# A macaron block on one core: an order table and a scatter loop changed in the second feed-forward pass

## What is computed

```python
x = x + 0.5 * _L0_ffn_ref(_layernorm(x, axis=-1), ...)
x = x + _L0_attn_ref(_layernorm(x, axis=-1), ...)
x = x + 0.5 * _L0_ffn_ref(_layernorm(x, axis=-1), ...)
```

```python
logits = x @ wr.T + rb
probs = jax.nn.softmax(logits, axis=-1)
scores, idx = jax.lax.top_k(probs, TOP_K)
scores = scores / scores.sum(axis=-1, keepdims=True)
...
out = shared_out
for e in range(E_ROUTED):
    out = out + w[..., e:e + 1] * _expert(x, rg[e], ru[e], rd[e])
```

## Time and profile before

| what | us |
|---|---|
| median of three runs (627.84, 629.61, 633.13) | 629.61 |
| the profiled execution | 629.03 |
| its span, first to last instruction | 627.2 |
| PE busy | 565.7 (90%) |
| DVE busy | 456.2 (73%) |
| ACT busy | 330.2 (53%) |
| POOL busy | 257.0 (41%) |

### The profile page before, as it was taken

How to read it: one execution, slowest core, us unless ns; L and a number is a source line. 1 busy time by engine, 2 the same in 40 slices (tenths; PEclk the granted TensorE clock), 3 DMA queues, 4 the chain that set the end, 5 groups by cost and what they waited for, 6 DMA issues and landing times.

```text
span 627.2 us, 11848 instructions
## 1 busy us (share of the span) xinstructions
PE 565.7 (90%) x3738; PEld 431.5 (69%) x3738; DVE 456.2 (73%) x1139; ACT 330.2 (53%) x703; POOL 257.0 (41%) x404
## 2 busy tenths in 40 slices
PE   2969999998895789999999999999999899899995
PEld 1859899997863455555555555555556898899894
DVE  3677777778558978787878787787555677577865
ACT  4444444457433346666666666566775524344543
POOL 7387846445333511212121212121316888744440
PEclk9999999999976989999999999999999979899998
DMA  9913237732571462505050404020000031421403
GB/s 261 279 44 82 74 96 185 189 103 72 159 224 54 148 136 68 159 2 160 1 158 2 157 2 158 4 92 1 3 2 22 31 83 48 115 73 41 121 31 106
DMA packets 46888, 58.74 MB, mean 94 GB/s; under 512 B 6183, under 2 KB 37678, under 8 KB 46062
## 3 DMA queue, kind: packets, MB, share of 16 engines
q1 hardware_dynamic: 38160, 46.77, 26.5%
q0 software_dynamic: 4480, 9.25, 4.7%
q10 hardware_dynamic: 4190, 1.98, 1.3%
HBM read 38.09 MB, written 28.00 MB: 105 GB/s over the span
## 4 chain that ended last, share of the span: by engine, by line
PE 66%; DVE 13%; issue 8%; DMA 4%; POOL 4%; ACT 3%; SPq 2%; DVEq 0%; ACTq 0%; POOLq 0%
PE psum L1566 11%; PE psum L1609 10%; PE psum L1631 10%; PE psum L846 4%; DVE mxp L1713 4%; PE psum L864 4%; PE psum L848 4%; PE psum L847 4%; PE psum L882 4%; PE psum L885 3%; DMA queries<-m_rows 2%; PE psum L1569 2%; POOL z_rows L1104 2%; PE psum L905 1%; DVE at_l L1005 1%
## 5 line engine op out<-in xcount | busy, mean ns | idle before, releaser
L1713 DVE TENSOR_REDUCE mxp<-psum 128x1 f32<-128x512 f32 (+3 forms) x304 | 182.8, 657 | 33.2 <-PE psum L1566 28.4
L1770 ACT ACTIVATE probs<-psum 128x512 f32<-128x512 f32 (+1 forms) x304 | 154.8, 580 | 97.9 <-PE psum L1609 79.6
L1566 PE MATMUL psum<-keys,queries 128*128 128x512 f32 (+1 forms) x304 | 118.3, 450 | 4.3 <-DVE mxp L1713 3.6
L1821 POOL TENSOR_SCALAR_AFFINE_SELECT probs<-probs 128x512 f32<-128x512 f32 x64 | 40.8, 638 | 175.2 <-ACT probs L1770 175.2
L1609 PE MATMUL psum<-queries,keys 128*128 128x512 f32 (+3 forms) x384 | 105.1, 366 | 8.0 <-DMA queries<-m_rows 7.4
L1126 POOL DMA_INDIRECT y_rows<-ys,to_row x76 | 74.3, 978 | 90.4 <-DVE ys L1043 55.8
L954 ACT ACTIVATE silu<-psum 128x352 f32<-128x352 f32 x107 | 49.7, 465 | 107.8 <-PE psum L848 96.8
L999 DVE TENSOR_TENSOR act<-silu,psum 128x352 f32<-128x352 f32 x107 | 55.6, 520 | 51.7 <-ACT silu L954 33.4
L1609 PEld LDWEIGHTS psum<-queries,keys 128*128 128x128 f32 x384 | 65.5, 189 | 32.4 <-ACT probs L1770 16.4
L1566 PEld LDWEIGHTS psum<-keys,queries 128*128 128x128 f32 x304 | 57.3, 198 | 41.8 <-DVE mxp L1713 36.4
L1631 PE MATMUL psum<-probs,vg 128*32 128x512 f32 (+3 forms) x768 | 76.0, 494 | 0.3
(11 more groups left out here) (260 smaller groups left out, 1025.3 us busy)
## 6 DMA issues: line engine op xcount, KB each, us to landing
z_rows<-q_stack SPq DMA_DIRECT2D x12, 682.5 KB, 5.6
keys<-q_stack SPq DMA_DIRECT2D x12, 512.0 KB
keys<-k_stack SPq DMA_DIRECT2D x32, 128.0 KB, 5.6
queries<-q_stack SPq DMA_DIRECT2D x8, 512.0 KB, 4.9
zg_early<-z_rows SPq DMA_DIRECT2D x44, 65.0 KB
yc<-y_rows SPq DMA_DIRECT2D x10, 256.0 KB, 3.0
zg_late<-z_rows SPq DMA_DIRECT2D x32, 65.0 KB
k_stack<-zt_h SPq DMA_DIRECT2D x8, 256.0 KB, 2.9
```

The costliest lines, as they stand in the source:

```text
L1566: ins = e.matmul(dst, K.queries[u][:, i * P:(i + 1) * P], K.keys[u][:, heads[0]:heads[-1] + 1, k0 * P:(k0 + nb) * P], start=True, stop=Tru ...
L1713: e.tensor_reduce(K.mxp[:, heads[0]:heads[-1] + 1, i, which], scores, AX.X, ALU.max).then_inc(K.A["taken"], 1)
L1770: e.activation(K.probs[:, kt % 2, heads[0]:heads[-1] + 1, q0:q1], src, ACT.Exp, scale=SCALE).then_inc(K.A["ex"], 1)
```

## The change

In the second pass the pauses behind half 1's transfers are left out, and those behind first choices (r = 0) in half 0; pauses that stay write to the same place as before. Ahead of each half POOL waits for the last pause. The transposition of chunk 2's norm moves from behind the up product of step 3 to ahead of that of step 4, with ACT's high half one place later; the places of batch 1 move one step later on PE and DVE. ACT's load of the second-rank results moves from behind its loop to the end of step 52, and the mix of chunk 2 from behind DVE's loop to the end of step 54.

```diff
@@ sort_pool
-    pause_pool(K, f == 1 and t < HALF)
+    if f == 0 or r and t < HALF:
+        pause_pool(K, f == 1)
@@ sort_part_pool
     if first == 0:
+        rested_pool(K)
         if f == 1:
             e.wait_ge(K.blank_rows[f], 16 * FILLS * LOOPED)
@@ the tables
-BETWEEN_ACT = [{46: (("q1", 0),), 48: (("q", 0), ("q1", 1)), 50: (("q", 1),)}, {3: (("norm_hi", 2),)}]
+BETWEEN_ACT = [{46: (("q1", 0),), 48: (("q", 0), ("q1", 1)), 50: (("q", 1),)}, {}]
-              {2: (("z", 2),), 3: (("z", 3),), 4: (("norm_hi", 3),), 20: (("tanh", 0),), 38: (("weigh", 0),), 40: (("weigh", 1),)}]
+              {2: (("z", 2),), 3: (("norm_hi", 2), ("z", 3)), 4: (("norm_hi", 3),), 20: (("tanh", 0),), 38: (("weigh", 0),), 40: (("weigh", 1),), 52: (("results", 1),)}]
-TAIL_PE = {2: (("proj", 2), ("proj", 3)), 7: (("places", 1),)}
-BETWEEN_PE = [{}, {1: (("proj_tr", 2), ("proj_tr", 3)), 3: (("norm_tr", 2),), 4: (("logits", 2), ("norm_tr", 3)), 5: (("logits", 3),)}]
+TAIL_PE = {2: (("proj", 2), ("proj", 3)), 4: (("norm_tr", 2),), 8: (("places", 1),)}
+BETWEEN_PE = [{}, {1: (("proj_tr", 2), ("proj_tr", 3)), 4: (("logits", 2), ("norm_tr", 3)), 5: (("logits", 3),)}]
@@ late_act
+    elif step == "results":
+        results_load(K, K.nc.scalar, f, c, (1,))
@@ the scalar block
             ffn_act(K, 1)
-            results_load(K, e, 1, 1, (1,))
             weigh_act(K, 1, 2)
             weigh_act(K, 1, 3)
@@ the vector block
             ffn_dve(K, 1)
-            mix_dve(K, 1, 2)
             mix_dve(K, 1, 3)
```

More of the change, by code:

```diff
@@ L2037 @@
               {0: (("proj_lo", 2), ("proj_lo", 3)), 1: (("x", 2), ("stats", 2), ("x", 3), ("stats", 3)), 3: (("norm_lo", 2),), 4: (("norm_lo", 3),),
-               5: (("router", (1, 0)), ("router", (1, 1))), 6: (("places", 1),), 8: (("segments", 1),), 9: (("lists", (1, 0)),),
+               5: (("router", (1, 0)), ("router", (1, 1))), 7: (("places", 1),), 8: (("segments", 1),), 9: (("lists", (1, 0)),),
                10: (("lists", (1, 1)),), 11: (("lists", (1, 2)),), 12: (("lists", (1, 3)),), 22: (("weights", 0),),
-               38: (("mix", 0),), 40: (("mix", 1),)}]
+               38: (("mix", 0),), 40: (("mix", 1),), 54: (("mix", 2),)}]
 FRONT_POOL = {26: 0, 28: 1}
-TAIL_PE = {2: (("proj", 2), ("proj", 3)), 7: (("places", 1),)}
-BETWEEN_PE = [{}, {1: (("proj_tr", 2), ("proj_tr", 3)), 3: (("norm_tr", 2),), 4: (("logits", 2), ("norm_tr", 3)), 5: (("logits", 3),)}]
+TAIL_PE = {2: (("proj", 2), ("proj", 3)), 4: (("norm_tr", 2),), 8: (("places", 1),)}
+BETWEEN_PE = [{}, {1: (("proj_tr", 2), ("proj_tr", 3)), 4: (("logits", 2), ("norm_tr", 3)), 5: (("logits", 3),)}]
 TAIL_ACT = {0: (("gather", 2), ("gather", 3), ("proj", 2), ("proj", 3))}
```

## The result

The changed kernel takes 642.19 us (median of 4 runs, 641.1 to 643.1) against 630.87 for the kernel before in the same session: a ratio of 1.0182, 95% interval 1.0130 to 1.0234. The forecast was 623.4, range 620.8 to 627.3. The profiled execution has a span of 641.1 us, 13.9 more than before.

A forecast was written before the change was run, and what follows sets the result against it. PE was taken to bound the second pass, losing time to waits and the half-clock stretches behind them, with batch 3 late through POOL's scatters. Sum: 629.0 - 4.1 (step 19) - 1.5 (tail) = 623.4 us, range 620.8 to 627.3.

The forecast's parts named there:

- Pauses: POOL's scatters: without pauses 1.27 us apart instead of 1.57, 0.30 saved for each pause; bounds 0.97 and 1.57 us.
- Norm transposition: Chunk 2's norm on PE: moved work fills the 1.27 us wait at 489.79; 0.8 us reaches the choice of experts.
- wait for batch 0: PE ahead of step 9: a new wait of some 2.5 us, until 509.6, unless the clock drops at 504.
- Places: Counting product one step later: idle time turned over, not removed; slots ready at 507.2 instead of 506.0, half 1 near 507.5.
- Steps 9 and 19: PE's rows of batches 0 and 3: start at 509.6 and 535.3, batch 3 ready at 533.0, gain 4.1 us.
- Tail: End of the pass: earlier load of second-rank results and earlier mix of chunk 2 gain 1.5 us.
- rule of the Trainium skill: Tail loads: DMAs from different engines share the same 16, so an earlier start buys no bandwidth; at worst 623.8 us.
- The slower one: Rival: bare scatters back up at POOL or in the DMA queue, batch 3 late; 633.8 us at 2.0 us each; chance 0.04.
- five rivals: No slow stretch or shorter scatter step (0.21), clock stays low (0.16), pauses idle (0.14), slower (0.04), tail turns (624.0 us).

The follow-up runs named there:

- e3: Kernel before with the pauses of half 1 alone taken out, half 0's kept: 641.22 us.
- e2: Changed kernel with all pauses of the kernel before put back, its other changes kept: 629.41 us, ratio to before 0.9996.
- e4: Kernel before with the tail's two moves alone: 628.74 us, ratio to before 0.9979.
- f4: Kernel before with the tail's two moves alone, measured again with more rounds: 628.71 us, ratio to before 0.9972.
- e1: Kernel before with only the pauses taken out as in the change (half 1's, and half 0's behind first choices): 645.29 us.
- e8: Kernel before with two full pauses behind each transfer of half 1, transfers 2.03 us apart: 637.50 us.
- e9: Kernel before with the tail's two moves and a second pause of 64 columns behind each full one of half 1: 631.51 us.
- f2: Kernel before plus 12 unpaused transfers by slot lists behind half 1, of 64 rows each instead of 128: 647.24 us.
- e5: Kernel before with half 1's pauses cut from 384 to 64 columns, transfers 1.29 us apart: 643.54 us.
- e12: Kernel before plus 12 unpaused transfers by slot lists behind half 1, of 128 rows each: 644.63 us.

## Why the prediction was wrong

**Pauses: the step that failed.** The spacing of bare transfers, 1.27 us, was right to the hundredth. Wrong was the term "0.30 saved for each pause": that a pause has only a time. I bounded its price by 0.97 and 1.57 us a transfer and asked whether transfers would back up "at POOL or in the DMA queue"; as evidence against I took that a scatter stays at 0.97 us. It still does in every kernel here. What backs up doesn't show in POOL's row: without half 1's pauses alone (e3) PE's signals come up to 14 us late and the pass is 11.9 us longer, where this term and what follows from it were to gain 4.1. The Trainium skill has a sentence on this in "Perfetto Trace Analysis", section "DMA Instruction — SWDGE (GPSIMD)": for transfers whose descriptors POOL makes itself, the profiler's end is the moment when the descriptors have been made, not when the DMA engines have moved the data. The trace agrees: the row lasts 0.97 us, the completion is seen 2.28 us behind its start.

The sign was in the trace of before, in rows that I passed over because ACT isn't the bound: the product that ends at 522.19 (521.86 and 0.33) gets its silu at 523.23, 1.04 us late, though ACT is idle.

```profile
521.86 0.33 PE L848 MATMUL psum<-wall,zs_l 128*128 x1
```

```profile
523.23 0.47 ACT L954 ACTIVATE silu<-psum 128x352 f32<-128x352 f32 x1 [2.27 <-PE psum L848]
```

Through half 1 of before there are eight such starts, 0.2 to 1.05 us late, two more just behind it, and none in the pass ahead of 516. At 1.76 and 2.03 us a transfer they are gone. I asked of the pause "what waits for it" (nothing), not "what gets through during it".

**Norm transposition: right.** In e2, where only it can act, step 6's silu comes 17.5 us behind the first against 18.1 before: 0.6 gained, 0.8 forecast. It is spent at the wait for batch 0, as forecast, and batch 3 isn't earlier for it.

**Places: right in kind, half 1's start mis-sized.** Forecast were slots 1.2 us later and half 1 about where it started. With the pauses back (e2) the slots are ready 25.5 us behind the first silu against 24.0 before, 1.5 later; POOL starts 0.81 us behind them, where 0.3 was counted; and half 1 starts 26.3 us behind the first silu against 25.6 in e4 and f4, 0.7 later. In the changed kernel the start at 513.76 instead of 507.5 is late signals behind half 0's pairs, as here 3.7 us behind a product that ends at 500.51; e1, with places unmoved, has the late start too (515.65).

```profile
500.19 0.32 PE L848 MATMUL psum<-wall,zt_late_l 128*128 128x352 f32 x1
```

```profile
504.26 0.46 ACT L954 ACTIVATE silu<-psum 128x352 f32<-128x352 f32 x1 [4.61 <-PE psum L848]
```

**Steps 9 and 19: never came about.** PE's rows of batch 0 start at 514.47 instead of 509.6, and the 24.4 us of work behind them were torn by the late signals. The 4.1 us of gain became 15.2 us of loss (13.8 over the pass, and the tail's 1.4 on top). That batch 3 is what PE waits for, and at what price, was right (e8, e9).

**Tail: right.** 1.5 us forecast; 1.4 in the changed kernel, 1.5 in e2, e4 and f4 (last silu to the end: 11.6 us before, 10.2, and 10.05 in these three). The loads lie inside the cover, and the four at once are in time:

```profile
629.62 0.99 ACTq L1200 DMA_DIRECT2D yc<-y_rows  x2
630.92 0.46 ACT L954 ACTIVATE silu<-psum 128x352 f32<-128x352 f32 x1 [1.48 <-PE psum L848]
...
634.10 1.28 ACT L1073 ACTIVATE yc<-yc,w 128x128 f32<-128x128 f32 x4 [1.04 <-DMA yc<-y_rows]
635.79 1.28 ACT L1073 ACTIVATE yc<-yc,w 128x128 f32<-128x128 f32 x4 [0.41 <-DMA yc<-y_rows]
```

The silu starts 0.3 us behind the issues. Chunk 2 is there 4.5 us behind the first issue, chunk 3 before 635.79. By the rule of the Trainium skill that the prediction names ("DMA: Bandwidth & Descriptors", section "Issuing engines are not separate DMA queues"), at its worst, the gain would have been 1.1. The trace agrees that the loads share the engines (4.5 us from ACT's issue to the first scaling, against 3.0 before, 617.54 to 620.58 in the earlier trace rows), but the earlier start paid in full.

**The rivals.** The slower one was told in the right words and bound to the wrong place: "back up" was to show as a spacing from 1.68 us on, and it had 0.04 of the chance. None of the five rivals held a wait for PE's own signals.

## What to carry to other kernels

An instruction that does nothing may be there for what gets through while it runs: before taking it out, look at all engines beside it, the idle ones too, for starts that are late behind finished work. Keep transfers by list from POOL apart while PE's products are waited for (here, with 128 rows of 520 bytes, 1.57 us still left up to 1.05 us of delay through half 1 of before, and 1.76 none), or use plain ones where no list is needed. And where two ends of a trade meet (here late signals below 1.57 us, a late batch above), the gain is to be looked for elsewhere, as in the tail.

## What was not expected of the hardware

- PE's signals came up to 16 us late while POOL issued transfers by list 1.27 us apart (18 in f2, 1.20 apart); in the same stretch DVE's and ACT's reached PE and DVE in 0.02 to 0.14 us (0.02 and 0.06 in the rows above). PE's come in PE's order, and the last in a burst, 2.6 to 2.9 us behind the last transfer where no other follows (after, e1, e3, e5). In e12, where scatters 1.57 us apart follow, one is held for 11 us longer (546.31 to 557.57): at that spacing what has piled up seems hardly to be worked off.
- In before the ten late starts lie at two places of a transfer's step: 0.66 us behind the transfer's start (two), or 1.40 to 1.46 us behind it (eight), which is between the end of the pause and the next transfer. The silu at 523.23 above is one of the eight:

```profile
521.81 0.97 POOL L1104 DMA_INDIRECT z_rows<-zrow_late,slots  x1 [0.16 <-issue]
522.78 0.43 POOL L1113 MEMSET idle<- 128x384 bf16 x1
```

So a signal that is held seems to get through at two moments of each step, one of them behind the pause; why there, no run here tells.

- A transfer by list costs POOL 0.96 us for 128 rows and 0.90 for 64, with 0.30 between two; plain ones of the same 128 rows follow each other in 0.53.
- Open: through which part POOL's work on lists and PE's signals run together; no run here shows it, nor whether the product's last write is late with the signal, since the profile models a product's end. Nor is it explained why 15 transfers, 0.3 us too close each, make delays of 15 us.
